# Attention in eight-head-band groups: the products with V in six pairs of units instead of ten bursts, with a fifth slot for probabilities

## What is computed

```
qkv = clip(layernorm(x) @ Wqkv.T, -8, 8);  q = ln(q) * q_w + q_b;  k = ln(k) * k_w + k_b
scores = q @ k.T / 4 + slope[h] * (j - i)         # causal: j <= i
x = x + softmax(scores) @ v @ Wout.T
x = x + layernorm(x) @ sum_k(alphas[k] * bases[k]).T
```

## Time and profile before

| what | value |
|---|---|
| median of the runs (lowest, highest) | 746.62 us (745.32, 748.37) |
| the profiled execution, and its span | 747.09 us, 745.4 us |
| TensorE busy | 677.8 us, 91% of the span |
| VectorE busy | 571.7 us, 77% |
| ScalarE busy | 410.8 us, 55% |
| mean TensorE clock granted | 0.95 of full speed |

### The profile page before, as it was taken

The page is one execution under the profiler, slowest core; times in us unless marked ns, Lnnn a source line. Parts: engine busy times, 40 slices in busy tenths (PEclk is TensorE's granted clock), DMA queues, the critical chain, the costliest instruction groups (busy, mean ns, idle before and its releaser), DMA issues.

```text
span 745.4 us, 16038 instructions
## 1 busy us (share of the span) xinstructions
PE 677.8 (91%) x6096; PEld 413.6 (55%) x6096; DVE 571.7 (77%) x990; ACT 410.8 (55%) x855; POOL 312.7 (42%) x403
## 2 busy tenths in 40 slices
PE   3999999993929799999999999999999999499998
PEld 3888888871305354445544554455455443378886
DVE  6798899973938688999898999999889830177664
ACT  4133322331007687878777888788788887222221
POOL 1477677773111262452652633123222323543540
PEclk9999999995558999999999999999999999699999
DMA  8325555564686334334423433343434201544442
GB/s 288 86 77 160 153 163 171 155 176 135 189 203 173 108 111 125 93 105 121 128 85 115 123 103 106 112 127 95 120 99 122 72 24 36 136 129 138 138 139 85
DMA packets 102828, 93.64 MB, mean 126 GB/s; under 512 B 12408, under 2 KB 82680, under 8 KB 102752
## 3 DMA queue, kind: packets, MB, share of 16 engines
q1 hardware_dynamic: 100640, 90.52, 42.3%
q0 software_dynamic: 2112, 2.10, 1.2%
HBM read 57.44 MB, written 33.82 MB: 122 GB/s over the span
## 4 chain that ended last, share of the span: by engine, by line
PE 58%; SPq 17%; DMA 10%; DVE 5%; issue 5%; POOL 2%; ACT 2%; DVEq 0%; POOLq 0%; ACTq 0%
PE ps L1069 18%; PE ps L1104 16%; SPq L401 9%; PE ps L1050 7%; PE ps L984 5%; PE ps L986 4%; PE ps L985 4%; SPq L434 4%; DMA second_q<-shift_lo 4%; DMA x_in<-in_x 2%; SPq L485 2%; PE ps L1046 2%; ACT probs L753 2%; PE ps L992 1%; DVE qk_stat L868 1%
## 5 line engine op out<-in xcount | busy, mean ns | idle before, releaser
L923 DVE TENSOR_REDUCE stats<-ps 128x1 f32<-128x512 f32 (+3 forms) x608 | 359.2, 656 | 67.2 <-PE ps L1050 65.5
L753 ACT ACTIVATE probs<-ps 128x512 f32<-128x512 f32 (+2 forms) x640 | 309.5, 559 | 92.8 <-PE ps L1069 92.6
L1050 PE MATMUL ps<-first_k,first_q 54*128 54x128 bf16 (+3 forms) x1152 | 220.0, 284 | 14.4 <-issue 11.4
L1069 PE MATMUL ps<-first_q,first_k 54*128 54x512 bf16 (+3 forms) x768 | 195.4, 329 | 24.0 <-DMA second_q<-shift_lo 19.9
L1069 PE MATMUL ps<-second_q,second_k 64*128 64x128 bf16 (+4 forms) x1152 | 205.0, 274 | 0.0
L650 POOL TENSOR_SCALAR_AFFINE_SELECT probs<-probs 128x256 f32<-128x256 f32 x256 | 103.0, 408 | 140.3 <-ACT probs L753 133.2
L1104 PE MATMUL ps<-probs,v_sb 128*32 128x512 f32 (+3 forms) x1536 | 157.9, 498 | 1.6 <-issue 0.8
L1069 PEld LDWEIGHTS ps<-first_q,first_k 54*128 54x128 bf16 x768 | 57.5, 94 | 137.3 <-ACT probs L753 112.5
L1050 PEld LDWEIGHTS ps<-first_k,first_q 54*128 54x128 bf16 x1152 | 92.5, 96 | 59.3 <-DVE stats L923 32.8
L1069 PEld LDWEIGHTS ps<-second_q,second_k 50*128 50x128 bf16 (+1 forms) x1152 | 92.0, 95 | 21.8 <-issue 1.7
L984 PE MATMUL ps<-wqkv_hi,xt_hi 128*128 128x512 f32 x192 | 77.1, 402 | 0.0
(11 more groups left out here) (79 smaller groups left out, 785.7 us busy)
## 6 DMA issues: line engine op xcount, KB each, us to landing
parts_dram<-parts SPq DMA_DIRECT2D x96, 128.0 KB, 2.2
v_dram<-v_ext SPq DMA_DIRECT2D x16, 512.0 KB, 3.5
v_sb<-v_dram SPq DMA_DIRECT2D x16, 512.0 KB, 4.3
o_dram<-o_sb SPq DMA_DIRECT2D x32, 256.0 KB
first_q<-parts_dram SPq DMA_DIRECT2D x96, 64.0 KB
first_k<-parts_dram SPq DMA_DIRECT2D x96, 64.0 KB
second_q<-parts_dram SPq DMA_DIRECT2D x96, 64.0 KB
second_k<-parts_dram SPq DMA_DIRECT2D x96, 64.0 KB
```

Source lines behind the costliest of these rows:

```text
L753: act.activation(weights, scores, ACT.Exp, scale=SCALE).then_inc(exp_done, 1)
L923: dve.tensor_reduce(to, scores, AX.X, ALU.max).then_inc(max_taken, 1)
L1050: last = pe.matmul(ps[:, bank, r * cols:(r + 1) * cols], first_q[n % STACKS][rows, hp, i * P:(i + 1) * P], first_k[n % STACKS][rows, hp, k ...
L1069: return pe.matmul(ps[:, bank, r * cols + first:r * cols + last], stack_k[n % STACKS][rows, heads[r] // PAIR, kb * P:(kb + 1) * P], stack_ ...
```

## The change

Products with V now run only when an odd unit is due, and then for the even unit before it as well: pairs (0, 1), (2, 3), (4, 5), (6, 7), (8, 9), (10, 11). The bursts stand after steps 13, 17, 25, 33, 1 and 5 (the last two in the next group). The number of slots for probabilities goes from four to five. Nothing else changes; every product is still computed, with the same shapes.

```diff
-P_SLOTS = 4
+P_SLOTS = 5
...
-NARROWEST = [u for u in range(NU) if unit_columns(u)[1] == P]
...
                     u = ENTRIES[e % NE][0]
-                    if e % NE == UNIT_END[u] and u + 1 not in NARROWEST:
-                        if u in NARROWEST:
-                            weigh(e // NE * NU + u - 1)
+                    if e % NE == UNIT_END[u] and u % 2:
+                        weigh(e // NE * NU + u - 1)
                         weigh(e // NE * NU + u)
```

## The result

The changed kernel takes 764.71 us, the median of four runs (763.04 to 769.85), against 746.65 us before in the same comparison. The ratio is 1.0252 with a 95% interval of 1.0199 to 1.0305: it is slower by 18 us, well outside the scatter of the runs. The forecast was 767, with a range of 751 to 778. The profiled execution has a span of 762.8 us, 17.4 more than before.

The account below looks back on a forecast made before the run. TensorE was taken as the bound, with VectorE close behind through its ring of three banks. Groups 1 to 13 (13.0 us), the other groups (3.5) and the shift loads (3.5) added 20.0 to 747.1: 767 us, range 751 to 778.

Parts of the forecast that it names:

- the loads of the shift: Weight-shift loads needed by step 40: 0.57 us less time to land, taken as 3.5 us in all, bounds 0 and 9.
- Fewer boundaries: Four burst boundaries per group go, each with a fixed 0.15 us on TensorE: gain of 0.60 us per group.
- Steps 26 to 33: Eight 512-wide steps paced by VectorE's ring: 3.87 us until the burst instead of 3.30, loss 0.57 per group.
- Steps 18 to 25: Diagonal steps waiting for VectorE and the last mask product: 4.29 us against 3.91, loss 0.38 per group.
- Steps 6 to 13: ScalarE holds TensorE, as step 13 needs step 9's exponential: 3.37 us against 2.76, loss 0.61 per group.
- Steps 34 to 41: Four narrow pieces and one step without: 2.69 us against 2.65, loss 0.04 per group.
- The last group: ScalarE-limited end: about 0.9 us idle behind a double burst, 0.6 for each of five pairs, 3.0 us.
- The fifth slot: One more slot for probabilities: costs nothing, and its wait never ends last.
- Rival 1: Boundaries decide and VectorE catches up in longer runs: faster, 731 to 737 us, centre 735; chance 0.13.
- Rival 2: Both cancel: waits grow 0.8 us per group, 0.6 comes back, shift loads unchanged: 747 to 751 us; chance 0.10.
- Rival 3: Shift loads bound most groups: up to 16 wait, 9 us, giving 773 to 778; chance 0.15 shared with another rival.
- Rival 4: ScalarE's shortfall after double bursts exceeds VectorE's beyond steps 6 to 13: 0.3 us more per group, 771; shared chance 0.15.

## Why the prediction was right

The direction and the mechanism held: VectorE and ScalarE pace the longer runs of steps, and this costs more than the saved boundaries bring. That the time came within 3 us of the forecast is luck in part: a group lost 1.48 us and not 1.00, and the shift loads gave time back instead of costing some, two errors that nearly cancel. The kernel of ten bursts with V's load moved has no waits for the shift loads beyond the first, like the changed kernel, so the two spans, 739.8 and 762.8 us, differ by what the pairs cost alone: 23.0 us. (Both are single executions; repeats of either kernel lie some 2 us apart or more.) Minus the 5.6 us of waits that the changed kernel sheds, this is the measured 17.4.

| term | forecast | measured |
|---|---|---|
| groups 1 to 13 | 13 x 1.00 = 13.0 | 13 x 1.48 = 19.2 |
| groups 0, 14 and 15 | 3.5 | the rest, 23.0 - 19.2 = 3.8 |
| the loads of the shift | +3.5 | -5.6 |
| sum | 20.0 | 17.4 |

- **Fewer boundaries**: 0.60 forecast, 0.55 measured in the bursts, and 0.61 per period where both other engines do half their work. The reading of the fixed 0.15 us from bursts of one and two units was right. No run shows what the 0.15 us consists of. The prediction puts its 10.6 us on the third rival's side, a slip: it is the first rival's.
- **Steps 26 to 33**: 3.87 against 3.85. The chain goes over VectorE just as worked out; with VectorE at half its work ScalarE still holds them at 3.47.
- **Steps 18 to 25**: 4.29 against 4.35, and 3.85 with VectorE at half its work, so VectorE is the one though the chain does not name it. **Steps 6 to 13**: 3.37 against 3.47; the later copy confirms that ScalarE is the one.
- **Steps 34 to 41** is the term that was mis-sized: loss 0.04 forecast, 0.33 measured. I took 0.35 us from the last piece's issue to the burst, as in the earlier trace rows. That holds only when the step's first product was issued early and the step waits for its piece alone. Here ScalarE's ring holds that first product too, until the exponential of step 37 is done, so two 512-wide products are still to come, about 0.5 us, and the piece itself goes 0.1 later. That these steps keep their 3.00 us with VectorE at half its work bears it out. I had worked ScalarE's side through for one of the eights only.
- **The last group**: idle times of 0.9 us behind a double burst were forecast for ScalarE. They are 1.1 to 1.4, as in this row, where the earlier trace rows had 0.22:

```profile
641.78 3.81 ACT L752 ACTIVATE probs<-ps 128x512 f32<-128x512 f32 x8 [1.13 <-PE ps L1068]
```

- **The loads of the shift** are the step that failed. It took landings as fixed and only the cover as shrinking. The cover did shrink as worked out (0.56 us in SP's queue against 0.57), but the landings came sooner by more. The lower bound of 0, "if the longer groups let the queue run ahead", named the right mechanism but stopped short: the waits that existed were themselves part of what could go, so the lower end had to be -5.9.
- **The fifth slot**: costs nothing, as forecast. That it is not needed in the steady groups was not said.
- **A sign that did not show**: the waits of line 1049's weight loads were to more than double from 19.1 and reached 29.4. The period, the idle times behind the bursts and the chain all showed the mechanism. The row grew in steps 26 to 33 alone, where three waits of 0.20, 0.32 and 0.44 us stand in place of one of 0.25. Steps 34 to 41 and 6 to 13 are held by ScalarE, and in steps 18 to 25, which VectorE does pace, no weight load of line 1049 has a wait booked. So a growing wait need not grow in its old row.

Rival 1 fell with the period above 24.8; its condition, added waits below 0.6 us per group, was missed by more than three times (2.03 us). Its gain appears when both other engines do half their work. Rival 2 wanted 0.8 us of added waits per group and falls with the same 2.03. Rival 3's mechanism went the other way. Rival 4's figures were right about ScalarE in steps 34 to 41.

## What to carry to other kernels

While TensorE runs a burst whose results the others do not wait for, they work through their rings and then stand idle. In this kernel, where VectorE had work for 22.0 of a group's 24.8 us, that decided the sign. So compare its length plus the time to the first new result with banks times the consumer's pace: here 1.86 + 0.37 us against 3 x 0.60, where the single burst had 0.99 + 0.37. If it is longer and the consumer has little time to spare, joining two bursts can cost more than the fixed cost it saves. Between the bursts, work out for every run of steps when each consumer returns the bank that the last step needs, for each ring and not only for the one that is named most often. And look at loads that are waited for in some rounds only: the order in which one queue issues a large load and small urgent ones was worth 1% here.

## What was not expected of the hardware

Four small loads whose issue takes 2.5 us land at a median of 3.1 us with 512 KB issued 5.4 us before them, and 2.2 us with those issued 7.3 us before (both distances read in one group), and 2.3 us with those issued behind them.
